# Second LayerNorm of the feed-forward stage: its row broadcasts and its apply pass moved from before the first matmul to its end

## What is computed

```
def reference(x, W_in, W_state, W_dt, b_dt, A_log, W_C, D, W_out, w1, b1, w2, b2):
    x = layernorm(x + ssm(x, ...))          # stage A: projections, a scan over time, gate
    h = relu(fixed_quant(quantized_linear(x, w1, b1), 8, 4))     # 1024 -> 4096
    return layernorm(x + quantized_linear(h, w2, b2))            # 4096 -> 1024

def quantized_linear(x, w, b):
    return fixed_quant(x, 8, 4) @ fixed_quant(w, 8, 6).T + fixed_quant(b, 8, 6)

def fixed_quant(x, width, frac):            # round, clip, rescale
    return clip(round(x * 2**frac), -2**(width-1), 2**(width-1) - 1) / 2**frac

def layernorm(x):                           # over the 1024 features, eps 1e-5
    return (x - mean(x)) / sqrt(var(x) + eps)
```

## Time and profile before

| | |
|---|---|
| median of 3 runs | 3874.47 us (3872.6 to 3879.13) |
| the profiled execution, its own time | 3882.74 us |
| span of its slowest core in the profile (core 5) | 3867.7 us |
| spans of the eight cores | 3859.5 to 3867.7 us |
| part A and weight load | first 1,030 us or so |
| part B, one loop body | 88.8 us from one mm1 start to the next (30 of them: 88.4 to 89.0, the first 95.3) |
| PE busy, share of span | 76% |
| DVE busy, share of span | 55% |
| ACT busy, share of span | 7% |

### The profile page before, as it was taken

One profiled execution on the slowest core, in us unless ns is written; L12 is line 12 of the kernel. 1 busy time (PEld: TensorE's weight loads), 2 busy tenths in 40 slices (PEclk: granted clock), 3 DMA queues, 4 the chain that ended last, 5 costly groups with the idle time before them and its releaser, 6 DMA issues.

```text
span 3867.7 us, 54885 instructions; the slowest of 8 cores (3859.5 to 3867.7 us)
## 1 busy us (share of the span) xinstructions
PE 2939.0 (76%) x21120; PEld 2132.7 (55%) x21120; DVE 2136.4 (55%) x6420; ACT 281.8 (7%) x467; POOL 19.0 (0%) x26
## 2 busy tenths in 40 slices
PE   3999999950377777777777777777777777777787
PEld 1444444420266566665566665666665666666666
DVE  0344444447766655556666666555566666665555
ACT  1222222210000000000000000000000000000000
POOL 0000000000000000000000000000000000000000
PEclk9999999985588888888888888888888888888888
DMA  7123323225300000000000000000000000000000
GB/s 106 23 45 50 47 46 46 43 87 206 98 17 17 17 17 17 17 17 17 23 17 28 17 17 17 17 17 17 17 17 23 17 28 17 17 17 17 12 12 23
DMA packets 110192, 128.06 MB, mean 33 GB/s; under 512 B 4320, under 2 KB 102624, under 8 KB 108912
## 3 DMA queue, kind: packets, MB, share of 16 engines
q1 hardware_dynamic: 72320, 83.89, 6.7%
q0 software_dynamic: 20976, 23.89, 4.9%
q10 hardware_dynamic: 16640, 16.78, 1.9%
HBM read 98.07 MB, written 50.33 MB: 38 GB/s over the span
## 4 chain that ended last, share of the span: by engine, by line
PE 69%; DVE 23%; issue 3%; DMA 3%; another core or an unknown queue 2%; DVEq 1%; ACT 0%; ACTq 0%; SPq 0%
PE pb L205 60%; PE pb L202 9%; DVE htmp8b L673 3%; DVE htmp8b L680 2%; DVE hq_sb L686 2%; DVE x_sb L552 2%; DVE x_sb L546 2%; DVE htmp8b L624 2%; DVE htmp8b L629 2%; DVE xq_sb L635 1%; DVE sqb L600 1%; DMA wstage_b<-w2T 1%; DVE sqb L501 1%; DMA wstage_b<-w1T 1%
## 5 line engine op out<-in xcount | busy, mean ns | idle before, releaser
L205 PE MATMUL pb<-xq_sb,w1q 128*128 128x256 bf16 x7168 | 960.6, 284 | 4.1 <-DVE htmp8b L673 4.1
L205 PE MATMUL pb<-hq_sb,w2q 128*128 128x256 bf16 x7936 | 953.5, 283 | 12.4 <-DVE hq_sb L686 12.4
L205 PEld LDWEIGHTS pb<-hq_sb,w2q 128*128 128x128 bf16 x7936 | 799.4, 101 | 151.6 <-issue 35.8
L205 PEld LDWEIGHTS pb<-xq_sb,w1q 128*128 128x128 bf16 x7168 | 727.7, 102 | 134.5 <-issue 25.2
L588 DVE SCALAR_TENSOR_TENSOR r_sb<-pb,b2q,x_sb 128x256 bf16<-128x256 f32 x256 | 123.8, 484 | 865.8 <-PE pb L202 865.8
L205 PE MATMUL pb<-xb,winT_sb 128*128 128x512 bf16 x1792 | 430.6, 380 | 63.2 <-DMA xb<-xT 63.2
L673 DVE TENSOR_SCALAR htmp8b<-pb,b1q 128x256 f32<-128x256 f32 x1024 | 424.8, 477 | 40.7 <-DVE hq_sb L686 31.4
L202 PE MATMUL pb<-row,ones_row 1*128 1x256 f32 x256 | 109.5, 549 | 361.9 <-DVE row L519 359.8
L205 PEld LDWEIGHTS pb<-xb,winT_sb 128*128 128x128 bf16 x1792 | 175.1, 98 | 276.6 <-issue 70.2
L202 PE MATMUL pb<-xq_sb,w1q 128*128 128x256 bf16 x1024 | 288.2, 281 | 0.0
L205 PE MATMUL pb<-sqb,ones_bf 128*1 128x256 bf16 x448 | 82.4, 342 | 254.0 <-DVE sqb L501 229.0
(11 more groups left out here) (87 smaller groups left out, 1853.7 us busy)
## 6 DMA issues: line engine op xcount, KB each, us to landing
outT<-ob SPq DMA_DIRECT2D x32, 1024.0 KB, 4.5
xb<-xT POOLq DMA_DIRECT2D x16, 1024.0 KB, 16.0
r1s<-r_sb ACTq DMA_DIRECT2D x16, 1024.0 KB, 7.5
r1ld<-r1s SPq DMA_DIRECT2D x32, 512.0 KB, 4.0
wstage_a<-w1T SPq DMA_DIRECT2D x4, 2048.0 KB, 8.1
wstage_b<-w1T SPq DMA_DIRECT2D x4, 2048.0 KB, 8.5
wstage_a<-w2T SPq DMA_DIRECT2D x16, 512.0 KB, 3.4
wstage_b<-w2T SPq DMA_DIRECT2D x16, 512.0 KB, 3.4
```

Of the source, the lines that this page charges most:

```text
L205: E.matmul(o, l, r, **kw))
```

## The change

The rows of LN2 (`rows_and_s`) stay where they are in DVE's queue. The two LN2 broadcasts on PE are emitted after the seventh mm1 subgroup (gsub 6), and the LN2 apply (16 DVE instructions and the store) after the eighth, ahead of the squares for the next tile. In a body without mm1 (the last) everything stays as it was.

```
+            ln2_rows = [None]
             if do3:
-                rows2_vd, sv2 = rows_and_s(bm2, bv2, tvm2, tvv2, rows2)
-                bmb2, brs2, tvrs2 = emit_bcasts(rows2, rows2_vd, sv2)
+                ln2_rows[0] = rows_and_s(bm2, bv2, tvm2, tvv2, rows2)
+
+            def emit_ln2_rows():
+                rows2_vd, sv2 = ln2_rows[0]
+                return emit_bcasts(rows2, rows2_vd, sv2)
+
+            def emit_ln2_apply(bcasts):
+                bmb2, brs2, tvrs2 = bcasts
                 if t3 >= 1 and out_store[t3 - 1] is not None:
                     wait("V", "qo", out_store[t3 - 1])
                 src2 = [r2_sb[:, c, :] for c in range(DC)]
...
                 out_store[t3] = dma("Y", "qo", dstap, ob[:, :, :],
                                     pre=[("vd", apply2_vd)])
+
+            if do3 and not do2:
+                emit_ln2_apply(emit_ln2_rows())
             if do2:
                 p2 = t2 % 2
                 hq_vd = None
...
                     prev_ts3[0] = hq_vd
+                    if gsub == 6 and do3:
+                        ln2_bcasts = emit_ln2_rows()
                 state[t2]["hq_vd"] = hq_vd
+                if do3:
+                    emit_ln2_apply(ln2_bcasts)
             if 0 <= it + 2 < NTB and "sq1_vd" not in state[it + 2]:
                 emit_sq1(it + 2)
```

## The result

The changed kernel takes 3767.8 us (median of all 9 runs, 3764.3 to 3903.6) against 3880.2 us before (median of all 10); the ratio is 0.9714, 95% interval 0.9703 to 0.9725. That is 112 us, 2.9%, faster. I had forecast 3877 and called no change the likeliest. The ratio and every time and comparison from here on leave out the runs in which the cores of one die or of both showed a lower clock than in the others (two on either side, the 3903.6 is one); the rest have medians of 3766.8 and 3879.4.

The account below looks back on a forecast made before the run. The prediction took PE and DVE to bound the kernel in turns, neither full. Full bodies +10.7 us, last bodies -10.2, plus 2 for broadcasts and the slowest core made +2.5: a median of 3877 us, range 3861 to 3904.

Parts of the forecast that it names:

- (a): Start of mm1: PE begins when xq is ready, 0.14 us after quantization ends instead of 3.71 us later.
- (b): First mm1 subgroup: DVE meets PE at the start, so PE paces its four groups at the low clock, 5.6 us.
- the stretch: End of quantization, through mm1, to the squares' release of PE: DVE sets the pace, 42.62 us against 41.90.
- (c): Rest of mm1: 0.29 and 2.42 us around the first subgroup's end, 26.91 for seven others; broadcasts before the last are hidden.
- (d): End of mm1: the LN2 apply, 5.49 us, delays the squares in DVE's first-in-first-out queue; then 1.85 us to PE's release.
- The clock in mm2: mm2's first group, slow at the low clock, takes 4.85 us against 5.2: -0.35 us per full body.
- The last bodies: Bodies 30 and 31 get shorter by 4.6 and 5.6 us, together -10.2 us.
- Rival 1: Earlier clock rises after the starts of mm1 and mm2 absorb the delay; only the tail's -10.2 stays: 3864 us, chance 0.14.
- the ring: The repeating loop body, 88.8 us long before the change.
- Rival 2: Start of mm1: without broadcasts to wake PE, four groups take 5.9 to 6.8 us; 3905 us, slower; chance 0.23.
- Rival 3: End of mm1: the apply leaves the path, not holding squares or mm2, 5.4 us less per body: 3716 us, chance 0.03.
- Rival 4: Start of mm1: the clock costs nothing, four groups take 3.49 us instead of 5.6: 3824 us, chance 0.03.

Follow-up runs that it names:

- e1: Changed kernel, with PE made to wait ahead of mm1 for this body's quantization (tile t1), which it does not need: 3875.3 us, ratio to before 0.9999.
- e4: Changed kernel, with the squares for the next tile emitted ahead of the LN2 apply: 3665 us, ratio to before 0.9451.
- e6: Changed kernel, with eight extra squares per body on DVE ahead of those PE waits for: 3817 us (a single value).
- e6b: Changed kernel, with four extra squares per body on DVE ahead of those PE waits for: 3784.8 us, ratio to before 0.9768.
- e7: Changed kernel, with the squares ahead of the LN2 apply and the LN2 broadcasts behind the eighth mm1 subgroup instead of the seventh: 3613 and 3622 us.
- e3: Changed kernel, with LN2 broadcasts and apply back at the front, only mm1's first subgroup of PE groups ahead of them: 3865.1 us, ratio to before 0.9971.
- e9: Changed kernel, with 92 extra unused matmuls on PE between mm1 and the squares' matmuls: 3716.0 us, ratio to before 0.959.
- e5: Changed kernel, with LN2 broadcasts after the third mm1 subgroup and the apply after the fourth: 3838.7 us, ratio to before 0.9897.

## Why the prediction was wrong

**The step that failed is (a): "It can begin when xq is ready ... so mm1 starts 0.14 after 2198.06".** mm1 of a body reads tile t2, whose quantization was done one body earlier; the xq that ends at 2198.06 is tile t1's, for the next body. My own description of the loop says so, and the wait in the code is on `state[t2]["xq_vd"]`. I read the end of quantization in the timeline as a release because PE's start lay behind it, yet the bracket on that row names line 519, not line 635, and line 519 was the wait that the change removes. In the changed kernel PE starts 8.74 us before that point and is held by banks alone.

**(b) fell with it.** The first subgroup was to be paced by PE at the low clock, 5.6 us. It took DVE's own 1.64. Without that term the stretch is 1.29 (to the first line 683) + 3.66 (first subgroup, as 2207.44 to 2211.10 in the earlier trace rows) + 26.91 - 0.08 + 5.49 + 1.85 = 39.12; measured 39.25. The other terms of the stretch held, and e1, which adds the wait I had assumed, ran in 3875.3 against my 3877: the arithmetic was right for another kernel. That it came so close is in part luck. In e1 DVE's stretch was 42.94 against my 42.62, and mm2 gave back 0.70 us a body against my 0.35; the two misses cancel.

**(c) and (d) held.** The broadcasts took 1.16 us at the high clock and cost nothing, the apply followed 0.08 us ahead of line 696's end, and the squares behind it. The apply is on the path, 5.4 us of it: e4 took it off and the squares' matmuls came 5.3 us earlier. The rule of the Trainium skill that I weighed there ("TensorE: Matmul & The Clock Gate", section "Architectural detail: the array is 16× 32×32, not 1× 128×128": DVE's queue is strictly first in, first out) agrees with the timelines: the squares ran behind the apply after the change and ahead of it in e4, as emitted.

**The clock in mm2.** I took -0.35 us per body; it was -0.68. Right in sign, half in size. Over the ten kernels with the change or a variant of it and without extra matmuls, mm2 took 30.3 to 31.3 us in the mean, which is up to 30 us of a run, and I could not have fixed it closer than that.

**The last bodies.** I had -10.2; they gave -14.2. Body 31 was right (-5.6 both): with no t1 it is the one body in which PE does meet DVE at the start, as (b) had it for all. Body 30 gave -8.6 for -4.6, again because the first subgroup was not held.

**The rivals.** Rival 1 (the ring keeps its length) is refuted for mm2's slow start by e6 and e6b; for both slow starts together e1 speaks against it, whose bodies ran from 88.6 to 90.3 us. Rival 2 needed the wait that isn't there; in e1, which has it, the first four groups of mm1 took 5.71 us in the mean, below the 6.1 that was to decide for it. (Before the change, 13 of the 30 middle bodies had the longer start of mm1, not 12; nothing hangs on it.) Rival 3, the apply off the path, is not what happened, but e4 and e7 show that a swap of two steps makes it happen; together with PE's early start that gave 3665 and 3613, below the 3716 that I had for it alone. Rival 4 came nearest in its reason (no slow start of mm1) and missed the other half, that the groups lie ready before DVE is there. The one that I lacked was the plain one: PE was held by nothing but the broadcasts.

What is shown: that PE's start ahead of the quantization's end is necessary for the gain (e1), that it isn't enough (e3), what the remaining low clock costs (e9). What stays open: why mm2's slow part settles where it does in each kernel.

## What to carry to other kernels

When a wait is removed, list what else the released instruction waits for, by tile and body, from the code's own wait and not from what ends just before it in the timeline; in a software pipeline the same buffer name stands for another tile. Then ask which engine's queue sets each stretch: here moving 5.4 us of DVE's work under PE's stretch gave 5.3 us a body, while moving it within DVE's stretch gave only the gap it had caused. Count the banks that a broadcast holds until it is read: two of eight cost 1.8 us of DVE's stretch in the middle of mm1 and nothing at its end.

## What the runs showed of the hardware

PE's rest before mm2 cost 1.8 us per body through the low clock alone, and 92 useless matmuls took it away (e9), so more matmuls made the kernel 51 us faster. In the changed kernel PE paused three times for 1.6 to 1.8 us between 2155 and 2168 and the granted clock stayed at 1.00; after rests of 6.0 us (e5) and 10.5 us (e1) it started at the low level. In mm1 of the kernel before the low clock cost next to nothing, since DVE had the apply to do meanwhile, and at the broadcasts ahead of it some 0.5 us a body (2.53 us of waiting against 2.00 in body 31). So the page's rise from 8 to 9 tenths is mostly time that was hidden.
